# Output projection of an attention kernel: products with features on the partitions, in three passes of split operands, one place later in the round

## What is computed

```
xn = layernorm(x)                                   # x: 4 x 1024 x 128
q, k, v = xn @ Wq, xn @ Wk, xn @ Wv                 # 16 heads of 64
w = softmax(q k^T / 64 + causal)                    # per head, 1024 x 1024
w = w * clip((key_no + span * 1024) / 33, 0, 1);  w = w / (sum(w) + 1e-8)
attn = concat_heads(w @ v) @ Wo                     # Wo: 1024 x 128
xq = clip(round(xn / scale), -127, 127) * scale
out = x + attn + (xq @ (ternary - 1)^T + bias)
```

## Time and profile before

| | |
|---|---|
| time, median of 3 runs | 1000.46 us (1000.36 to 1007.18) |
| the profiled execution, its own time | 1000.45 us |
| its span | 998.7 us |
| outside of the span | 1.75 us |
| busy share of the span | PE 98%, DVE 76%, POOL 71%, PEld 63%, ACT 45% |
| granted TensorE clock | full, all through |

### The profile page before, as it was taken

One profiled execution on the slowest core, in us unless ns is written; L12 is line 12 of the kernel. 1 busy time (PEld: TensorE's weight loads), 2 busy tenths in 40 slices (PEclk: granted clock), 3 DMA queues, 4 the chain that ended last, 5 costly groups with the idle time before them and its releaser, 6 DMA issues.

```text
span 998.7 us, 19217 instructions
## 1 busy us (share of the span) xinstructions
PE 983.3 (98%) x7125; PEld 633.6 (63%) x7125; DVE 756.3 (76%) x1706; ACT 451.4 (45%) x607; POOL 706.4 (71%) x649
## 2 busy tenths in 40 slices
PE   8999999999999999999999999999999999999997
PEld 4565666666666666666666666666666666666654
DVE  7877888878788878787767777777777667777754
ACT  4444445444444444454443454443454444454442
POOL 8766767767767667867766767667767667777672
PEclk9999999999999999999999999999999999999999
DMA  6000000000000000000000000000000000000000
GB/s 177 3 2 2 2 1 3 2 3 2 2 22 3 2 2 2 1 2 2 2 12 13 1 3 2 2 2 3 1 2 23 3 2 2 1 3 2 2 2 22
DMA packets 16133, 8.52 MB, mean 9 GB/s; under 512 B 5404, under 2 KB 15644, under 8 KB 16040
## 3 DMA queue, kind: packets, MB, share of 16 engines
q1 hardware_dynamic: 15416, 7.15, 2.6%
q10 hardware_dynamic: 624, 0.14, 0.1%
HBM read 4.33 MB, written 2.10 MB: 6 GB/s over the span
## 4 chain that ended last, share of the span: by engine, by line
PE 86%; DVE 9%; issue 2%; POOL 1%; ACT 1%; DMA 1%; DVEq 0%; SPq 0%; ACTq 0%; POOLq 0%
PE pv L1025 25%; PE ring L1008 23%; PE ring L970 12%; PE beside L1067 7%; PE beside L1040 6%; DVE ring L770 3%; PE ring L943 3%; PE ring L939 3%; PE ring L940 3%; DVE v L757 3%; DVE beside L794 1%; PE beside L1055 1%; PE beside L977 1%; PE ring L957 1%; PE ring L958 0%
## 5 line engine op out<-in xcount | busy, mean ns | idle before, releaser
L569 ACT ACTIVATE prob<-ring 128x1024 f32<-128x1024 f32 (+3 forms) x384 | 293.6, 810 | 346.7 <-PE ring L1008 346.6
L503 POOL TENSOR_TENSOR psumd<-psumd,prob 128x512 f32<-128x512 f32 (+1 forms) x250 | 406.2, 1625 | 28.9 <-POOL psumd L503 1.3
L770 DVE CUSTOM_DVE_ANT_0 ring<-ring,causal 128x128 f32<-128x128 f32 (+3 forms) x512 | 240.4, 517 | 97.1 <-PE ring L970 96.3
L1008 PE MATMUL ring<-q,k 64*128 64x512 f32 (+3 forms) x2304 | 279.8, 347 | 2.3 <-DMA mrow<-maxrow 0.8
L1025 PE MATMUL pv<-prob,v 128*64 128x512 f32 (+3 forms) x1536 | 267.1, 490 | 0.0
L476 POOL TENSOR_SCALAR_AFFINE_SELECT prob<-prob 128x256 f32<-128x256 f32 x256 | 109.4, 429 | 217.0 <-ACT prob L569 214.9
L1008 PEld LDWEIGHTS ring<-q,k 64*128 64x128 f32 x2304 | 194.6, 185 | 37.6 <-DVE rowmax L770 5.2
L1025 PEld LDWEIGHTS pv<-prob,v 128*64 128x64 f32 x1536 | 104.9, 137 | 154.1 <-issue 142.0
L774 DVE TENSOR_REDUCE rowmax<-ring 128x2 f32<-128x1024 f32 x128 | 151.4, 1222 | 3.9 <-PE ring L970 0.5
L499 POOL TENSOR_TENSOR psumd<-prob 128x768 f32<-128x768 f32 (+1 forms) x63 | 132.5, 2103 | 24.2 <-ACT prob L569 19.1
L970 PE MATMUL ring<-k,q 64*128 64x512 f32 (+3 forms) x768 | 142.9, 408 | 3.0 <-DVE k L746 0.7
(11 more groups left out here) (120 smaller groups left out, 943.3 us busy)
## 6 DMA issues: line engine op xcount, KB each, us to landing
kext<-kext SPq DMA_DIRECT2D x128, 4.0 KB, 1.7
out<-x_sb SPq DMA_DIRECT2D x8, 256.0 KB, 2.4
x_sb<-in_L_attn_query SPq DMA_DIRECT2D x3, 512.0 KB, 5.5
mrow<-maxrow SPq DMA_DIRECT2D x62, 4.0 KB
x_sb<-in_L_attn_query SPq DMA_DIRECT2D x2, 256.0 KB, 4.3
xn_sb<-in_L_attn_Wv SPq DMA_DIRECT2D x1, 512.0 KB, 5.2
wo<-in_L_attn_Wo SPq DMA_DIRECT2D x1, 512.0 KB, 7.0
xn_sb<-in_L_attn_Wq SPq DMA_DIRECT2D x1, 448.0 KB, 3.5
```

The source lines that it names most:

```text
L503: g.tensor_tensor(acc[:, :, lo:HALF], acc[:, :, lo:HALF], pr[:, :, lo:HALF], ALU.add).then_inc(acc_done, 1)
L569: a.activation(prob[n % NPROB][:, :, lo:HALF], ring[:, slot(f"S{t}", i), :, lo:HALF], ACT.Exp, scale=1.0 / DH).then_inc(exp_done, 1)
L770: last = v.tensor_tensor_reduce(out=ring[:, s, h, 0:n], in0=ring[:, s, h, 0:n], in1=causal[:, HALF - n:HALF], scale=1.0, scalar=MASKED, op ...
L1008: last = t_.matmul(ring[:, s, h, lo:HALF], k[p][rows, keys], q[p][rows, cols], start=(at == 0), stop=(at == len(parts) - 1))
```

## The change

The output products are formed the other way round in all pairs but the last. Wo is split into `wo1`, `wo2` (high and low parts, fp32r), once, in round 0: ACT writes the high part, POOL the low part. A half's values are split too: `o_hi` by ACT (words `h0`, `h1`), `o_lo` by DVE (`l0`, `l1`). `Y` then is three matmuls with 128 x 128 weights from Wo and 512 moving columns, and the product has output features on the partitions. DVE adds it up over the eight pairs of a batch in `yt` (`Ya`; the first pair copies), and once per batch `P0`, `P1` turn the sums back with four transposes each on PE and DVE adds them to `x_sb`: in rounds 9, 17 and 25 and for the fourth batch, without its last pair, in round 31. The last pair keeps its fp32 products, with its rows of Wo in `wo_last`. `Y0` and `Y1` each stand one place later: pair i-1's `Y0` where `Y1` stood, pair i-1's `Y1` at the end of round i.

Memory is rearranged for that: `xn_sb` shrinks to three batches' worth of rows, its first third serves as `yt`, `o_sb` is one buffer, `lnden` goes (`ln` and `ex` work in place in `r0`), raw Wk lies in `prob[7]`, Wo is loaded ahead of the inputs of batches 1 to 3. The layer norm's last steps move from rounds 11, 12 to 16, 17, the bias of the fourth batch from 14 to 18, and the seven `q` steps one round later. A batch is stored after the turned sums are added.

```diff
-PE_PLAN = ("T Q+ K+ X0 X1 W G11- M0+ M1+ S0 S1 S2 M2+ D1- M3+ S3 V+ S4 S5 M4+ S6 M5+ Y1- M6+ M7+ S7 D0 G3 "
-           "M8+ S8 S9 S10 M9+ Y0 M10+ M11+ S11 G7")
-ACT_PLAN = "Z Qhi+ Khi+ X0 X1 E0 E1 E2 ln1- ex1- E3 E4 E5 E6 E7 ln0 ex0 E8 E9 E10 E11"
+PE_PLAN = ("T Q+ K+ P0 X0 X1 W G11- P1 M0+ M1+ S0 S1 S2 M2+ D1- M3+ S3 V+ S4 S5 M4+ S6 M5+ Y0- M6+ M7+ S7 D0 G3 "
+           "M8+ S8 S9 S10 M9+ Y1- M10+ M11+ S11 G7")
+ACT_PLAN = "Z Qhi+ Khi+ X0 X1 wo E0 E1 E2 ln1- ex1- E3 E4 E5 E6 h1- E7 ln0 ex0 E8 E9 E10 E11 h0"
-DVE_LAST = "Tc t1- u1- o1- A5 Ya1- A6 A7 t0 u0 o0 A8 A9 Ya0 t1 u1 o1 Ya1"
+DVE_LAST = "Tc l0- q Ya0- t1- u1- o1- P0 A5 l1- A6 Ya1- A7 t0 u0 o0 P1 A8 A9 Ya0 t1 u1 o1 Ya1"
...
+            def values_high(i, c):
+
+                act.wait_ge(o_done, halves_upto(i, c))
+                if halves_upto(i, c) > 1:
+                    act.wait_ge(y_ready, halves_upto(i, c) - 1)
+                a.activation(o_hi[:, :], o_sb[:, :], ACT.Copy).then_inc(o_hi_done, 1)
...
+            def values_low(i, c):
+
+                dve.wait_ge(o_hi_done, halves_upto(i, c))
+                v.tensor_tensor(o_lo[:, :], o_sb[:, :], o_hi[:, :].bitcast(F32), ALU.subtract
+                                ).then_inc(o_lo_done, 1)
...
+            def turn_back(i, c):
+
+                b = batch_turned_back(i)
+                pe.wait_ge(y_added, halves_upto(min(b * NPB + NPB - 1, LAST - 1), c))
+                for k in range(HB):
+                    n = c * HB + k
+                    last = t_.transpose(beside[:, k * P:(k + 1) * P], yt[:, n * P:(n + 1) * P], ident[:, :])
+                last.then_inc(turned_back, 1)
...
-                pe.wait_ge(o_done, halves_upto(i, c))
-                for k in range(HB):
-                    last = t_.matmul(beside[:, k * P:(k + 1) * P], o_sb[c][:, k * P:(k + 1) * P],
-                                     wo[:, i % NPB, :], start=not with_ffn, stop=(not with_ffn or k == HB - 1))
+                if i < LAST:
+                    if i == 0 and c == 0:
+                        pe.wait_ge(wo_lo_done, 1)
+                    pe.wait_ge(o_hi_done, halves_upto(i, c))
+                    w_hi, w_lo = wo1[:, i % NPB, :], wo2[:, i % NPB, :]
+                    t_.matmul(beside[:, :], w_hi, o_hi[:, :], start=not with_ffn, stop=False)
+                    t_.matmul(beside[:, :], w_lo, o_hi[:, :], start=False, stop=False)
+                    pe.wait_ge(o_lo_done, halves_upto(i, c))
+                    last = t_.matmul(beside[:, :], w_hi, o_lo[:, :], start=False, stop=True)
```

More of the change, by code:

```diff
@@ L82, in happens @@
     if name == "q":
-        return i % PAIRS_OF_BATCH < PAIRS_OF_BATCH - 1
+        return i % PAIRS_OF_BATCH > 0
+    if name in ("P0", "P1"):
+        return i == LAST or i % PAIRS_OF_BATCH == 1 and i > PAIRS_OF_BATCH
+    if name == "wo":
+        return i == 0
+    if name == "wl":
+        return i == 2
+    if name in ("h0", "h1", "l0", "l1"):
+        return i < LAST
     if name == "Z":
@@ L97, in walk @@
     seen = set()
-    for i in range(-1, N_PAIRS + 1):
+    for i in range(-1, N_PAIRS + 2):
         for word in (first if i < 0 else plan if last is None or i < LAST else last).split():
@@ L111 @@
 IN_RING = [("X", -2)] + [u for u in PE_ORDER if u[0][0] in "QKSMV" or u == ("D1", LAST)]
-IN_BESIDE = [u for u in PE_ORDER if u[0][0] in "THDYXWF" and u not in (("D1", LAST), ("Y1", LAST))]
+IN_BESIDE = [u for u in PE_ORDER if u[0][0] in "THDYXWFP" and u not in (("D1", LAST), ("Y1", LAST))]
 PLACE = {u: n for n, u in enumerate(IN_RING)}
@@ L510, in _ @@
                     add(i, int(name[1:]))
+                elif name == "wo":
+                    pool.wait_ge(wo_hi_done, 1)
+                    g.tensor_tensor(wo2[:, :, :].rearrange("p n d -> p (n d)"), yt,
+                                    wo1[:, :, :].rearrange("p n d -> p (n d)").bitcast(F32), ALU.subtract
+                                    ).then_inc(wo_lo_done, 1)
                 else:
@@ L596, in _ @@
                 turned_high(0, c, ring[:, slot("X", -2), c, :])
-            for name, i in walk(ACT_PLAN, ACT_FIRST):
+            for name, i in walk(ACT_PLAN, ACT_FIRST, ACT_LAST):
                 if name in ("Qhi", "Khi"):
@@ L611, in _ @@
                     turned_whole(0, int(name[2:]), ring[:, slot("X", -2), int(name[2:]), :])
+                elif name[0] == "h":
+                    values_high(i, int(name[1:]))
+                elif name == "wo":
+                    weights(wo1[:, :, :].rearrange("p n d -> p (n d)"), yt, wo_landed, 16, wo_hi_done)
                 elif name == "rest":
@@ L866, in _ @@
                     add_output(i, int(name[2:]))
+                elif name[0] == "l":
+                    values_low(i, int(name[1:]))
+                elif name[0] == "P":
+                    add_turned_back(i, int(name[1:]))
                 elif name == "q":
[L868 removed]
+                    quantise(i // NPB, i % NPB)
                 elif name[0] == "X":
@@ L1053, in feed_forward @@
                 pe.wait_ge(fq_step, (i // NPB + 1) * FQ_STEPS)
+                if i < LAST:
+                    t_.matmul(beside[:, :], ternT[:, :], fq[:, c * HALF:(c + 1) * HALF], start=True, stop=False)
+                    return
                 for k in range(HB):
@@ L1060, in output_projection @@
                 with_ffn = i % NPB == NPB - 1
-                if i == 0 and c == 0:
-                    pe.wait_ge(wo_landed, 16)
                 if with_ffn and (f"F{c}", i) not in PLACE_BESIDE:
                     feed_forward(i, c)
-                pe.wait_ge(o_done, halves_upto(i, c))
-                for k in range(HB):
-                    last = t_.matmul(beside[:, k * P:(k + 1) * P], o_sb[c][:, k * P:(k + 1) * P],
-                                     wo[:, i % NPB, :], start=not with_ffn, stop=(not with_ffn or k == HB - 1))
+                if i < LAST:
+                    if i == 0 and c == 0:
[6 more added lines that the diff above has]
+                    last = t_.matmul(beside[:, :], w_hi, o_lo[:, :], start=False, stop=True)
+                else:
+                    pe.wait_ge(wo_last_landed, 16)
+                    pe.wait_ge(o_done, halves_upto(i, c))
+                    for k in range(HB):
+                        last = t_.matmul(beside[:, k * P:(k + 1) * P], o_sb[:, k * P:(k + 1) * P],
+                                         wo_last, start=not with_ffn, stop=(not with_ffn or k == HB - 1))
                 last.then_inc(y_ready, 1)
@@ L1103, in _ @@
                     idle_products(2 * P)
+                elif name[0] == "P":
+                    turn_back(i, int(name[1:]))
                 elif name[0] == "F":
```

104 lines of the change are left out of this document (73 added, 31 removed).

## The result

| | before | after |
|---|---|---|
| median | 1000.41 us (20 runs, 1000.22 to 1007.18) | 1006.60 us (20 runs, 1006.09 to 1014.13) |
| ratio, 95% interval | | 1.0069 (1.0052 to 1.0086) |
| the profiled execution | 1000.45 us, span 998.7 | 1012.81 us, span 1011.1, mean granted clock 0.991 |

The changed kernel is 6 us slower: forecast 1004, range 994 to 1011. Some executions of either kernel have a stretch at half clock near the start and take 6 to 8 us more (2 of 20 before, 4 of 20 after), and the profiled one of after is such an execution; what follows leaves its start out, and eleven of the twenty runs, without such a stretch, lie between 1006.09 and 1006.86.

The account below looks back on a forecast made before the run. PE, busy for 98% of the span, was taken as the bound. Gains 8.4 + 0.5 = 8.9, losses 1.3 + 2.5 + 4.3 + 4.5 = 12.6, net 3.7 slower: 1000.45 + 3.7 = 1004 us, range 994 to 1011 (8 in 10).

Parts of the forecast that it names:

- The products, the entry: Each Y on PE falls from 1.09 to 0.89 us, still paying 0.20 for entry from half-height to full-height work.
- no entry: Rival: the new Y form pays no entry, gaining 0.40 per second half; 998 us, or 992; chance 0.14.
- 8.4 gained: Rounds 1 to 30: 0.08 from the first Y and 0.20 from the second, 30 x 0.28 us.
- 1.3 lost in ordinary rounds: l0- on DVE pushes R0, and so S1, by 0.08 us in 16 ordinary rounds.
- The division between the halves: Of 0.20 us per Y, the first passes on 0.08 since S7 waits for R5; the second passes on all.
- Heavy rounds, 2.5 lost: Rounds 2, 3, 8, 10, 16, with norm or statistics steps: no idle DVE time before R0; bounds 1.5 and 4 us.
- `S1` by about 0.5: In rounds with norm or statistics steps, l0- pushes R0 by its full 0.60 us and S1 by about 0.5.
- Turning back, 4.3 lost: Rounds 9, 17, 25: transposes cost PE 1.1 us each, plus delays of R0; bounds 3.3 and 6 us.
- the 0.45 more in rounds 9 and 17: Extra loss per round there, as DVE's added work makes R0 later in rounds that have a norm step.
- the low part slows DVE: Rival: low parts take 0.98 us, delaying S1 and l1-'s followers; together 9.4, 1013 us; slower side beyond 1008 has 0.17.
- Round 31, 4.5 lost: Last round: D1- and P0 come later, D0 starts 4.4 us later behind Ya1-, P1's addition costs 0.1; bounds 3 and 5.5.
- Round 0, 0.5 gained; the start, 0: Round 0 loses its Y0 (1.09 us) but M10 waits for E9; splitting Wo fits in ACT's and POOL's idle time.

Follow-up runs that it names:

- Experiment 3: The kernel before, its fp32 products kept, with Y0 and Y1 each one place later and the q steps one round later: 1001.41 us.
- experiment 1: The changed kernel run once more, unaltered, for a trace without the half-clock stretch near the start: 1006.84 us, ratio 1.0065.
- experiment 8: The changed kernel without the turning back in rounds 9, 17 and 25, that part of the result left out: 1003.07 us.
- experiment 5: The changed kernel with the low parts of rounds 0 to 30 on POOL (GpSimd) instead of DVE: 1004.06 us.
- experiment 4: The changed kernel with POOL's bias add of rounds 6, 11 and 18 moved from the round's end to behind its fourth sum: median 1008.40 us.
- experiment 9: The changed kernel with l1- of rounds 1 to 30 reading its first operand from PSUM, plus an added wait for ACT's ex0: 1006.71 us.

## Why the prediction was right, and where its terms were off

The direction, the size class and the range were right; 1004 forecast, 1006.2 in undisturbed executions. Term by term:

- **The products, the entry.** Right: 0.90 measured for 0.89. The rival "no entry" is dead (its 0.69 would show as three equal records).
- **8.4 gained, 1.3 lost in ordinary rounds.** 0.28 less 0.08 in each of 16 rounds; measured 0.18 to 0.27. Experiment 3 shows that it is the form. The division between the halves was argued; the 0.31 us that `S7` waits in 28 rounds agree with it. Low parts met by no add take 0.67 to 0.68 (27 of 62).
- **Heavy rounds, 2.5 lost.** Mis-sized: rounds 2, 3 and 10 are as short as the ordinary ones (-0.18, -0.25, -0.18), hence 0. The step that failed is "`S1` by about 0.5": in rounds 3, 8 and 10 of experiment 1 `R0` starts 0.4 later behind `T` and the loads of `S1` wait 0.35 for it, but `V` starts only 0.02 to 0.06 later, so little of it was on the path. What did count is where the norm steps stand, for which the sum had no term: round 11, whose step has gone, gained 0.3 more, and rounds 16 and 17, which have steps now, lost about 0.25 each.
- **Turning back, 4.3 lost.** 3.5 by experiment 8. The 1.1 of PE per round is right (1.0); of the 0.45 more in rounds 9 and 17 no more than 0.1 arrives in the difference, although `l0-` does reach the path there: off DVE it gives 0.37 back in each, and none in round 25 (experiment 5).
- **What held the low parts was missing from the sum.** Rounds 1, 7, 12, 19 and 8, 16, 24 lose 5.5 us by it (experiment 5, which takes the low part off DVE; experiments 4 and 9 take away only the add in flight or the operand, and give 5.0 back in six of the seven rounds). The prediction had the rule as a rival, "the low part slows DVE", from the row of 1.96, and failed in two steps. It took that row for a rate, 0.98 for 512 elements, when it is a wait: an instruction with both operands in SBUF waits until POOL's add in flight is over, and what it costs is what is left of that add, 0.1 to 2.2 us, whatever its own size. The row itself shows it. DVE's sum starts at 972.77 and ends at 974.73, 1.09 behind this add of POOL, of which 0.87 was left (timeline of before, round 31); the same sum takes 1.23 where no add is in flight.

```profile
972.37 1.27 POOL L503 TENSOR_TENSOR psumd<-psumd,prob 128x512 f32<-128x512 f32 x1
```

And for `l0-` it looked for POOL's traffic in an ordinary round, where there is none, and gave `l1-` beside POOL's sums 0.98 at most. The price is paid where `l1-` starts just behind the start of `A6`, and where a bias add or the split of Wo stands at the end of a round.

- **Round 31, 4.5 lost.** 4.6. `D1-` to `D0` 10.4 (10.5 forecast), and `D0` follows the end of `Ya1-` (987.35 + 0.68) by 0.06. `P0` waited 1.26 for `rden` as foreseen.
- **Round 0, 0.5 gained; the start, 0.** 0.3 and 0 (`T` of round 0 at 30.64 against 30.70).

So 2.5 + 0.8 of losses that weren't there hid most of 5.5 that weren't foreseen: that the total was closer than its terms is luck.

The Trainium skill has the rule in plain words: the page "SBUF — State Buffer", section "SBUF: two separate sides", says that VectorE and GpSimd share one pair of ports, that an instruction of VectorE with two SBUF inputs takes it exclusively against one of GpSimd that reads SBUF, and that the second to come waits out the first. The runs here agree: with an add in flight 0.69 with one operand in PSUM, 0.81 to 2.84 with none. Read before the sum was made, it would have turned the question from "how much slower" to "which add is in flight".

## What to carry to other kernels

An elementwise instruction costs more than its row when both its operands are in SBUF and GpSimd adds beside it: lay the two engines' timelines over each other for each kind of round, and price what is left of the add in flight, not a slower rate. Take one operand from PSUM, or put the instruction where GpSimd idles; moving the work to GpSimd turns the same wait round. A test that swaps an operand can bring a wait of its own with it: look at where the instruction now starts, and not only at how long it takes. And a gain per round of 0.2 us is easily lost in the few rounds that are unlike the others: count those first, the last one above all, where a wait may also take the clock down.
